# Half of the query and key transposes moved from TensorE to the DMA in a fused attention kernel

## The reference

```python
def _L0_cond_ref(x, emb, W_emb, b_emb, g_norm, W_qkv, g_q, g_k, W_out):
    scale, shift = jnp.split(emb @ W_emb + b_emb, 2, axis=-1)
    xn = _rms_norm(x, g_norm) * (1.0 + scale) + shift
    qkv = (xn @ W_qkv).reshape(b, n, 3, h, d)          # b 4, n 1024, h 16, d 64
    ...
    q = _rms_norm(q, g_q)
    k = _rms_norm(k, g_k)
    logits = jnp.einsum('bhqd,bhkd->bhqk', q, k) * d ** (-0.5)
    attn = jax.nn.softmax(logits, axis=-1)
    o = jnp.einsum('bhqk,bhkd->bhqd', attn, v)
    ...
    return o + o @ W_out
x = x + _L0_cond_ref(x, cond[:, None, :], ...)
x = x + causal_depthwise_conv(x, w=cond, b=b)          # 4 taps
```

## Time and profile before

| | |
|---|---|
| median of 3 runs | 2486.0 us (2485.43 to 2486.32) |
| the profiled execution | 2484.39 us, of which the span is 2482.6 us |
| granted clock of TensorE, mean | 0.988 of full speed |
| busy | PE 95%, DVE 84%, ACT 74%, POOL 26% |
| DMA queue q1, share of 16 engines | 92.1% |

### The profile page before, as it was taken

How to read it: one execution, slowest core, us unless ns; L and a number is a source line. 1 busy time by engine, 2 the same in 40 slices (tenths; PEclk the granted TensorE clock), 3 DMA queues, 4 the chain that set the end, 5 groups by cost and what they waited for, 6 DMA issues and landing times.

```text
span 2482.6 us, 54243 instructions
## 1 busy us (share of the span) xinstructions
PE 2365.0 (95%) x20794; PEld 1526.7 (61%) x20794; DVE 2090.6 (84%) x3368; ACT 1829.1 (74%) x2834; POOL 640.5 (26%) x451
## 2 busy tenths in 40 slices
PE   4799999999899999999999999999999999999899
PEld 0455555555466666666666666666666666666688
DVE  7768988888778888888888988888888888888876
ACT  5467778888777777878777787777777777777632
POOL 1122323332233222332232223233222222222100
PEclk9899999999999999999999999999999999999999
DMA  9999999999998989999999999989988888888971
GB/s 365 296 216 227 194 182 193 181 188 227 197 203 180 197 182 212 181 199 225 197 217 182 204 195 194 184 189 228 201 174 169 182 171 170 167 161 164 181 188 52
DMA packets 1234737, 484.99 MB, mean 195 GB/s; under 512 B 1139632, under 2 KB 1197872, under 8 KB 1232048
## 3 DMA queue, kind: packets, MB, share of 16 engines
q1 hardware_dynamic: 1234480, 481.53, 92.1%
HBM read 137.20 MB, written 56.66 MB: 78 GB/s over the span
## 4 chain that ended last, share of the span: by engine, by line
PE 63%; DVE 20%; issue 5%; ACT 4%; SPq 3%; DMA 2%; ACTq 0%
PE proj L1014 32%; PE scores L956 10%; DVE neg L1542 9%; PE values L975 9%; PE proj L1039 8%; DVE p_pair L1551 7%; ACT p_pair L1193 2%; SPq L762 2%; DVE bias L1545 2%; PE proj L1044 1%; PE misc L1056 1%; ACT late L1185 1%; DMA w_sb<-w_dram 1%; SPq L718 1%; PE values L990 1%
## 5 line engine op out<-in xcount | busy, mean ns | idle before, releaser
L1014 PE MATMUL proj<-w_sb,xn_sb 128*128 128x384 f16 x6144 | 1035.2, 327 | 24.4 <-DMA w_sb<-w_dram 14.1
L1185 ACT ACTIVATE late<-scores,bias,l_scale 128x1024 f32<-128x1024 f32 x512 | 617.3, 1206 | 347.9 <-DVE bias L1545 329.4
L1014 PEld LDWEIGHTS proj<-w_sb,xn_sb 128*128 128x128 f16 x6144 | 587.5, 98 | 428.5 <-issue 28.8
L1551 DVE TENSOR_TENSOR p_pair<-late,p_pair 128x1024 f16<-128x1024 f32 x512 | 616.8, 1246 | 125.9 <-ACT p_pair L1193 125.8
L1542 DVE TENSOR_REDUCE neg<-scores 128x1 f32<-128x1024 f32 x512 | 623.2, 1217 | 109.4 <-PE scores L956 106.3
L1193 ACT ACTIVATE p_pair<-late 128x1024 f16<-128x1024 f32 x512 | 511.7, 1052 | 0.0
L975 PE MATMUL values<-pT,v_pair 128*64 128x256 f16 x6144 | 390.9, 278 | 14.7 <-ACT inv_row L1253 14.7
L956 PE MATMUL scores<-late 64*128 64x512 f16 x3072 | 377.6, 379 | 15.4 <-ACT late L1185 13.1
L975 PEld LDWEIGHTS values<-pT,v_pair 128*64 128x64 f16 x6144 | 319.5, 111 | 94.8 <-issue 70.9
L1458 POOL TENSOR_TENSOR rs<-ms,power 128x16 f32<-128x16 f32 x63 | 183.0, 2905 | 403.6 <-DVE ms L1565 403.3
L1039 PE MATMUL proj<-late,wo 128*128 128x256 f16 x2304 | 267.7, 273 | 1.5 <-issue 1.5
(11 more groups left out here) (181 smaller groups left out, 2026.8 us busy)
## 6 DMA issues: line engine op xcount, KB each, us to landing
w_sb<-w_dram SPq DMA_DIRECT2D x121, 384.0 KB, 4.1
o_dram<-oT_pair SPq DMA_DIRECT2D x124, 128.0 KB, 2.4
out<-late SPq DMA_DIRECT2D x54, 256.0 KB, 2.9
x_in<-in_x SPq DMA_DIRECT2D x25, 512.0 KB, 4.5
late<-in_x SPq DMA_DIRECT2D x25, 512.0 KB, 4.2
wq_raw<-in_L_cond_W_qkv SPq DMA_DIRECT2D x8, 1536.0 KB, 10.7
late<-o_dram SPq DMA_DIRECT2D x12, 1024.0 KB, 6.0
xn_dram<-late SPq DMA_DIRECT2D x21, 512.0 KB, 3.6
```

Source lines behind the costliest of these rows:

```text
L1014: last = nc.tensor.matmul(proj[:, t % 2, 0:6 * DH], xn_sb[:, t, i * K + c, :], w_sb[:, c, j, :], start=(c == 0 and i == j == 0), stop=(c = ...
L1185: nc.scalar.activation(prob[:, h, :], scores[:, h, :], ACT.Exp, bias=bias[:, s:s + 1], scale=const["l_scale"][:, 0:1], accum_out=total[:, ...
L1551: nc.vector.tensor_tensor(p_pair[:, s % 4, 1, :], prob[:, h, :], p_pair[:, s % 4, 0, :], ALU.subtract).then_inc(lo_done, 1)
```

## The change

From w = 9 on (`by_dma(w)` is w > 8, so 23 of the 32 units' stacks), the stacks of half 0 are made by one DMA transpose, `transpose_qk`, in place of 16 TensorE transposes and two ACT copies. SP issues it at phase 5, right behind `transpose_p(u, 8)` and `(u, 9)`. Its 128 x 2048 float16 have the shape that `transpose_p` moves. `qk_pair` gets a buffer for each half, and `stack` is laid out so that one half of the tokens is contiguous. `score(u, 0)` waits on the new semaphore `st_in` where it waited on `h_ev`; `high_halves` and the counts of `h_tr` and `h_ev` follow. The SBUF for the second buffer comes from smaller or shared small tiles (`mod_rows`, `power`, `msx`, `y_tmp`). Half 1 stays on TensorE.

```diff
@@ main @@
-        qk_pair = sb("qk_pair", [P, 2, 2, KH, 2 * DH], F16)
+        qk_pair = sb("qk_pair", [P, 2, 2, 2, KH, 2 * DH], F16)
...
-        stack = late[:, 0:8192].rearrange("p (a j n) -> p a j n", a=2, j=4)
+        stack = late[:, 0:8192].rearrange("p (a f j n) -> p a f j n", a=2, f=2, j=4)
...
+        def by_dma(w):
+            return w > K
+
+        def reads(w):
+            return 3 * min(w, K + 1) + max(w - K - 1, 0)
+
+        def turns(w):
+            return 4 * min(w, K + 1) + 2 * max(w - K - 1, 0)
@@ SP @@
+            def transpose_qk(w, par):
+                sp.wait_ge(h_hi, 2 * w + 1)
+                sp.wait_ge(h_lo, 2 * w + 1)
+                need(sp, qk_done, NS * (w - 1))
+                sp.dma_start_transpose(stack[:, par, 0].rearrange("p j (t n) -> p (j t) n", n=P),
+                                       qk_pair[:, 0].rearrange("p j a t d -> p (j a t d)")).then_inc(st_in, 16)
...
+                    if qkv and by_dma(w) and p == 5:
+                        transpose_qk(w, 1 - par)
@@ TensorE @@
                 if p == 0:
-                    pe.wait_ge(h_ev, 3 * u + 2)
+                    if by_dma(u):
+                        pe.wait_ge(st_in, 16 * (u - K))
+                    else:
+                        pe.wait_ge(h_ev, 3 * u + 2)
                     pe.wait_ge(k_ev, u + 1)
...
-                        free1 = ((h_ev, 3 * w + 2) if qkv else (y_ev, 2 * T),)
+                        free1 = (((qkv_ev, K * w + 8) if by_dma(w) else (h_ev, 3 * w + 2)) if qkv else (y_ev, 2 * T),)
...
-                    if qkv and outs and p == 5:
+                    if qkv and outs and not by_dma(w) and p == 5:
                         stacks(w, 0, 0, misc[:], (f_ev, 2 * T if fins else 0))
                         stacks(w, 0, 1, proj[:, 1, :], (qkv_ev, K * w + 8))
@@ ACT @@
                 act.wait_ge(h_n, 2 * (2 * w + hf) + 2)
-                need(act, h_tr, 4 * w + 2 * hf)
+                if hf == 0 and by_dma(w - 1):
+                    act.wait_ge(st_in, 16 * (w - 1 - K))
+                else:
+                    need(act, h_tr, turns(w))
...
                         if qkv:
-                            read_stacks(w, 1 - par, 0, 0, 0, misc[:])
-                            read_stacks(w, 1 - par, 0, 1, 1, proj[:, 1, :])
+                            if not by_dma(w):
+                                read_stacks(w, 1 - par, 0, 0, 0, misc[:])
+                                read_stacks(w, 1 - par, 0, 1, 1, proj[:, 1, :])
```

More of the change, by code:

```diff
@@ L51, in late_chunk, with mod_rows_in @@
     return late[:, (c - FRONT) * size:(c - FRONT + 1) * size].rearrange("p (h s n) -> p h s n", h=K, s=2)
+def mod_rows_in(wo, B, K):
+    first = 2 * K * 12 * DH
+    return wo.rearrange("p c s n -> p (c s n)")[0:B * 2 * K, first:first + 2 * P].bitcast(F32)
 def wo_chunk(wo, c, K):
@@ L80, in bass_cond_attention_conv @@
             taps=sb("taps", [P, B, K], F32), conv_b=sb("conv_b", [P, K], F32),
-            power=sb("power", [P, 4 * K], F32),
+            power=sb("power", [P, 2 * K], F32),
             mod_two=sb("mod_two", [P, B], F32), mod_up=sb("mod_up", [P, B], F32),
@@ L463, in _ @@
             v.wait_ge(mod_t, 1)
-            nc.vector.tensor_copy(shared["mod_rows"][:], ps_e[0:B * 2 * K, 512:512 + P]).then_inc(mod_c, 1)
+            nc.vector.tensor_copy(mod_rows_in(wo[:], B, K), ps_e[0:B * 2 * K, 512:512 + P]).then_inc(mod_c, 1)
 def main(nc, const, shared, w_dram, mod_dram, xn_dram, o_dram, x, W_qkv, W_out, out):
@@ L578, in main @@
         h_ev = sem("h_ev")
+        st_in = sem("st_in")
         k_ev = sem("k_ev")
@@ L906, in unit @@
                             load_xn(u // K + 1, t)
-            sp.dma_start(mod_dram.rearrange("b i k p -> (b i k) p"), shared["mod_rows"][:]).then_inc(mod_out, 16)
+            sp.dma_start(mod_dram.rearrange("b i k p -> (b i k) p"), mod_rows_in(const["wo"][:], B, K)).then_inc(mod_out, 16)
             def second_w(first, last, source):
@@ L947, in score @@
                 if p == 0:
-                    pe.wait_ge(h_ev, 3 * u + 2)
+                    if by_dma(u):
+                        pe.wait_ge(st_in, 16 * (u - K))
+                    else:
+                        pe.wait_ge(h_ev, 3 * u + 2)
                     pe.wait_ge(k_ev, u + 1)
                 if p == KH:
-                    pe.wait_ge(h_ev, 3 * u + 3)
+                    pe.wait_ge(h_ev, reads(u + 1))
                 for i, j in ((0, 2), (0, 3), (1, 2)):
@@ L956, in score @@
                             last = nc.tensor.matmul(scores[:, h, n * HN:(n + 1) * HN],
-                                                    stack[rows_, par, i, p * P:(p + 1) * P],
-                                                    stack[rows_, par, j, n * HN:(n + 1) * HN],
+                                                    stack[rows_, par, p // KH, i, (p % KH) * P:(p % KH + 1) * P],
+                                                    stack[rows_, par, n, j, :],
                                                     start=(i == 0 and j == 2), stop=(i == 1))
@@ L1000, in project @@
                     elif t == (2 if early else 0):
-                        need(pe, h_ev, 3 * w)
+                        need(pe, h_ev, reads(w))
                     if fins is not None and t < 2:
@@ L1025, in stacks @@
                     for t in range(KH):
-                        last = nc.tensor.transpose(f16_bank[:, a, t * P:(t + 1) * P], qk_pair[:, j, a, t, :],
+                        last = nc.tensor.transpose(f16_bank[:, a, t * P:(t + 1) * P], qk_pair[:, hf, j, a, t, :],
                                                    const["eye16"][:])
@@ L1106, in unit @@
                             keep_clock(8)
-                        stacks(w, 1, 1, misc[:], (h_ev, 3 * w + 1))
+                        stacks(w, 1, 1, misc[:], (f_ev, 2 * T if fins else 0) if by_dma(w) else (h_ev, 3 * w + 1))
                         stacks(w, 1, 0, proj[:, 0, :], (y_ev, 2 * T + 1) if outs else
@@ L1227, in read_stacks @@
             def read_stacks(w, par, hf, j, count, bank, done=h_ev):
-                act.wait_ge(h_tr, 4 * w + count + 1)
-                nc.scalar.activation(stack[:, par, 2 * j:2 * j + 2, hf * HN:(hf + 1) * HN],
+                act.wait_ge(h_tr, turns(w) + count + (-1 if by_dma(w) else 1))
+                nc.scalar.activation(stack[:, par, hf, 2 * j:2 * j + 2, :],
                                      bank.bitcast(F16).rearrange("p (a n) -> p a n", a=2),
@@ L1405, in head_high @@
                     last = nc.scalar.activation(
-                        qk_pair[:, j, 0, t0:t1].rearrange("p t (h d) -> p (t h) d", d=DH),
+                        qk_pair[:, 1, j, 0, t0:t1].rearrange("p t (h d) -> p (t h) d", d=DH),
                         stage[:, 1, 2 * t0:2 * t1, j * DH:(j + 1) * DH], ACT.Copy)
@@ L1463, in half_low @@
                     last = nc.gpsimd.tensor_tensor(
-                        qk_pair[:, j, 1].rearrange("p t (h d) -> p (t h) d", d=DH),
+                        qk_pair[:, hf, j, 1].rearrange("p t (h d) -> p (t h) d", d=DH),
                         stage[:, hf, :, j * DH:(j + 1) * DH],
-                        qk_pair[:, j, 0].rearrange("p t (h d) -> p (t h) d", d=DH), ALU.subtract)
+                        qk_pair[:, hf, j, 0].rearrange("p t (h d) -> p (t h) d", d=DH), ALU.subtract)
                 last.then_inc(h_lo, 1)
@@ L1554, in read_keys @@
             def read_keys(w, par):
-                dve.wait_ge(h_tr, 4 * w + 3)
-                nc.vector.tensor_copy(stack[:, par, 2:4, HN:2 * HN],
+                dve.wait_ge(h_tr, turns(w) + (1 if by_dma(w) else 3))
+                nc.vector.tensor_copy(stack[:, par, 1, 2:4, :],
                                       misc[:].bitcast(F16).rearrange("p (a n) -> p a n", a=2)).then_inc(k_ev, 1)
@@ L1793, in head_low @@
                     last = nc.vector.tensor_tensor(
-                        qk_pair[:, j, 1, t0:t1].rearrange("p t (h d) -> p (t h) d", d=DH),
+                        qk_pair[:, 1, j, 1, t0:t1].rearrange("p t (h d) -> p (t h) d", d=DH),
                         stage[:, 1, 2 * t0:2 * t1, j * DH:(j + 1) * DH],
-                        qk_pair[:, j, 0, t0:t1].rearrange("p t (h d) -> p (t h) d", d=DH), ALU.subtract)
+                        qk_pair[:, 1, j, 0, t0:t1].rearrange("p t (h d) -> p (t h) d", d=DH), ALU.subtract)
                 return last
```

9 lines of the change are left out of this document (4 added, 5 removed).

## The result

| | before | changed |
|---|---|---|
| median of 22 runs each | 2486.11 us | 2491.34 us |
| lowest to highest | 2481.38 to 2492.27 | 2486.42 to 2496.69 |
| ratio of the changed kernel to before | | 1.002, 95% interval 1.0013 to 1.0027 |
| the profiled execution's span | 2482.6 us | 2489.1 us |

The change makes the kernel slower, by 5.2 us at the median, or 0.2%. The forecast was 2484.1 us, 1.9 us faster, with a range of 2478.5 to 2491.0.

The account below looks back on a forecast made before the run. The prediction took the last 12 us of each unit to be bound by DVE and ACT, not TensorE. Gains of 3.3 and 0.6 us against 2.0 of late weights took 2486.0 to 2484.1 us, range 2478.5 to 2491.

Parts of the forecast that it names:

- what of TensorE's time reaches the end: Maximum of phase 6: of 0.98 us freed on TensorE a unit, only 0.15 counts; 3.9 us gained with unit 8.
- The idle time foretold ahead of the scores of phases 7 and 0: Sign in the profile after: TensorE newly idle for about half a microsecond before those scores.
- The tie between TensorE's scores and DVE's L1577: Before phase 6's maximum in unit 20: scores ready at 1583.94, DVE free at 1583.86, so earlier scores gain only 0.15 us.
- what the DMA transpose costs by itself: At phase 5: 2.3 us of SP and of the DMA engines, landing 4.9 us after issue; its wait costs nothing.
- What queues behind it on SP: Later SP issues keep their places; DMA backlog delays quarter 3 of the weights, costing 2.0 us in all.
- the term of +2.0 us for late weights: TensorE waits for quarter 3 behind units 14 and 22 only, 1.0 us each, from their additional `load_xn`.
- The third assumption of the step: DMA rests of 1.6 us behind the insertion absorb part of its 2.3 us, leaving 0.7 when phase 7 comes.
- Rival 2: Rests unusable, so all 2.3 us reach quarter 3 of the weights: 14 us lost, 2496 us; chance 0.12.

## Why the prediction was wrong

**Right, with its size: what of TensorE's time reaches the end.** The step gave 0.15 us for each of 22 units and 0.6 us for unit 8. Measured: 0.17 and 0.66, together 4.4 us for the 3.9 foretold. By the medians of the kernel without the DMA transpose it is 3.1. The idle time foretold ahead of the scores of phases 7 and 0 is there too: the weight loads of `score` wait for ACT 45 times, 26.5 us in all, against 23 times and 7.7 us before. The tie between TensorE's scores and DVE's L1577 was the right place to look: the kernel without the DMA transpose and the one with TensorE's transposes back both confirm it.

**Right: what the DMA transpose costs by itself.** It lands 4.9 us after its issue, nobody waits on `st_in`, and it holds SP for 1.9 to 3.1 us where 2.3 were taken. The Trainium skill ("VectorE: DVE Perf Modes", The three transpose paths) gives 1309 ns for one 128 x 128 block by the DMA. The trace does not agree with 16 times that for one instruction of 16 blocks: they land in 4.9 us, the issue included.

**Wrong: "What queues behind it on SP", the term of +2.0 us for late weights.** It measured 7.8 us in the profile, and 8.4 as the difference of two medians. The place, quarter 3 of the weights at the 19th matmul, was named. Two things in the sizing failed:

- The step said "The later issues keep their places", with quarter 3 issued at 1595.45 in unit 20's terms. But a transpose behind loads holds SP until about the time at which they land, as shown above. Backlog does not just delay the landing of what is already issued; it delays the issue of all that stands behind the next transpose. Quarter 3 stood behind two such. Behind unit 8 it landed at 746.9, 7.3 us after the start of unit 9, against 3.6 in the kernel before: 3.7 us late, from a transfer sized at 2.3.
- One unit's slack, 2.0 us in unit 20, was taken for all ordinary ones, and a wait for the two with an additional `load_xn`. In the kernel before, quarter 3 landed 3.4 to 5.1 us after the start of the ordinary ones of units 9 to 30, and it is needed 6.1 us after it: the slack was 0.9 to 2.6 us. The two loaded units, behind units 14 and 22, cost 2.8 and 2.2 us, where 1.0 each was taken; three ordinary units cost 2.8 together, where nothing was.

The third assumption of the step, that the 1.6 us of rest are used whole and 0.7 us are left over, held in most units: in the 17 without a wait, quarter 3 landed 0.3 us later on average than in the kernel before. In the five with one it landed 1.8 to 3.8 us later.

**Rival 2 named the place and the direction, not the mechanism.** It gave 14 us, with all 2.3 us reaching quarter 3 in each of the 23 units. By the landings more than 2.0 us arrived in four units of 22. What was lost is 7.8 us in five units, by an issue held up there and not by rests that stay unused everywhere. With the gain of 4.4 that is +3.4 us; the medians show +5.2, an interval of 3.2 to 6.7. No rival had the case between: a small delay in most units and a long one in a few.

**What stays open.** Units 15 and 23 follow the two units with an additional `load_xn`, and in the kernel before their quarter 3 landed latest too, 6.0 and 5.5 us after the unit's start. Why units 9, 12 and 19 are late is open. In the stretch of unit 8 the new transpose landed 4.6 us behind the one ahead of it, while the others mostly took 2.4 to 2.9. One packet of queue q8, the instructions, fell into that stretch, and the rate sank to 41 GB/s there (DMA view, 722 to 731 us in 40 slices):

```profile
DMA  5019999999999999918959947999899916500000
GB/s 117 10 19 185 223 201 216 214 223 212 225 206 204 243 349 256 109 41 96 250 214 341 323 178 273 396 355 375 295 252 243 88 57 48 36 14 27 27 27 18
...
q8 instruction: 1, 0.02, 0.7%
```

But such a packet falls 14 to 16 us ahead of the start of each of units 9 to 30, those without a wait included, so that it is there does not tell the late ones from the others. Ahead of units 12 and 19 the new transpose landed as usual, and only the loads behind it came some 2 us later. That instruction loads set the jitter was not tried.

## What to carry to other kernels

Before you take work off the busiest engine, look at the first instruction behind it on the chain and ask when that one's own engine is ready: here DVE was free 0.08 us before TensorE, and so 0.98 us became 0.17. Then look for what has become the bound; one ACT instruction moved out of its way was worth 11 us, more than twice all that the change itself gained, and was a loss without it (2500.6 us against 2487.9). And when a transfer is put into a DMA queue, check the slack of everything that stands behind it in the worst unit, not in a typical one: above all a load queued behind transfers whose issue holds the queue. Issue a load that is needed early ahead of them, as soon as its buffer is free.

## What the runs showed of the hardware

The issue of a DMA transpose on SP is not a fixed cost: a pair held it for 4.60 us with idle DMA engines and for 7.70 us behind 0.75 MB of loads, in which time SP issued nothing else. Of the transposes right behind a load, the 20 that held SP longest in the two kernels, 4.0 to 6.3 us, each let it go 0.05 to 0.55 us before that load landed. And the prologue with units 0 to 7 varies by 6.9 us from profile to profile, in no order of the kernels, while the steady units of one kernel repeat within 0.02 us; a difference of a few microseconds is better read from the units than from one span.
